# Local attention over smaller score tiles: 8 heads by 16 queries by 48 positions

## The reference, cut to what matters

```
idx = 1 + arange(t_pad)[:, None] + arange(L)[None, :]      # L = 32 positions seen by each query
uk, uv = recK[:, :, idx], recV[:, :, idx]                   # E = 4 records per position
Q = einsum('ntc,hdc->nhtd', X, w_Q)                         # H = 8 heads, DK = 64
scores = einsum('nhtd,netld->nhtel', Q, uk) / sqrt(DK)
probs = softmax(scores over the E * L = 128 keys)
Y = einsum('nhtel,netld->nthd', probs, uv)
return Y @ w_O
```

## Time and profile before

| | us |
|---|---|
| span of the profiled execution | 1794.7 |
| median of 3 runs | 1796.14 (1792.08 to 1797.33) |
| PE busy | 1657.5 (92% of the span) |
| PEld busy | 1273.5 (71%) |
| DVE busy | 1000.5 (56%) |
| ACT busy | 643.1 (36%) |
| POOL busy | 509.4 (28%) |

### The profile page before, as it was taken

One profiled execution on the slowest core, in us unless ns is written; L12 is line 12 of the kernel. 1 busy time (PEld: TensorE's weight loads), 2 busy tenths in 40 slices (PEclk: granted clock), 3 DMA queues, 4 the chain that ended last, 5 costly groups with the idle time before them and its releaser, 6 DMA issues. The chain is left out here.

```text
span 1794.7 us, 31966 instructions
## 1 busy us (share of the span) xinstructions
PE 1657.5 (92%) x10524; PEld 1273.5 (71%) x10524; DVE 1000.5 (56%) x2537; ACT 643.1 (36%) x1913; POOL 509.4 (28%) x655
## 2 busy tenths in 40 slices
PE   8999899999999987778789999998999997999998
PEld 6777677777778755667678888886666665656555
DVE  6545457777777877896632222216888885322221
ACT  3333255554545465345521111112444443111110
POOL 3222210000000066785243333315444441100000
PEclk9999899999999999889789999999999998999999
DMA  7776500000000000000423333312111100000000
GB/s 192 133 150 114 99 13 13 13 13 14 12 12 1 2 16 1 17 24 32 149 54 96 108 107 100 94 53 97 31 30 32 30 24 1 12 12 12 23 12 24
DMA packets 92269, 88.53 MB, mean 49 GB/s; under 512 B 11456, under 2 KB 82048, under 8 KB 91776
## 3 DMA queue, kind: packets, MB, share of 16 engines
q1 hardware_dynamic: 73392, 56.63, 13.2%
q0 software_dynamic: 6912, 18.88, 3.9%
q10 hardware_dynamic: 11856, 11.66, 1.9%
HBM read 46.64 MB, written 23.20 MB: 39 GB/s over the span
## 5 line engine op out<-in xcount | busy, mean ns | idle before, releaser
L845 ACT ACTIVATE probs<-psS,nm 128x256 f32<-128x256 f32 x256 | 119.1, 470 | 182.4 <-DVE nm L878 182.4
L1790 DVE COPY YE<-e_psY 128x512 f32<-128x512 f32 x40 | 27.7, 691 | 227.7 <-PE e_psY L1738 227.7
L1728 PE MATMUL e_psH<-e_XT,w 128*128 128x256 f32 x640 | 144.8, 379 | 0.0
L1738 PE MATMUL e_psY<-w,e_HT 128*128 128x256 f32 x640 | 144.5, 379 | 0.0
L876 DVE TENSOR_REDUCE mx<-psS 128x2 f32<-128x512 f32 x128 | 87.8, 686 | 84.2 <-PE psS L766 81.9
L1738 PEld LDWEIGHTS e_psY<-w,e_HT 128*128 128x128 f32 x640 | 121.6, 190 | 16.5
L766 PE MATMUL psS<-Rec,QT 128*128 128x256 f32 (+1 forms) x512 | 132.3, 381 | 0.9 <-ACT QT L833 0.9
L1766 ACT ACTIVATE e_HT<-e_psH 128x512 f32<-128x512 f32 x80 | 47.7, 597 | 235.9 <-PE e_psH L1728 235.9
L1728 PEld LDWEIGHTS e_psH<-e_XT,w 128*128 128x128 f32 x640 | 118.6, 190 | 14.5
L1696 POOL DMA_INDIRECT XE<-token_rows,held x80 | 76.0, 950 | 184.7 <-PE e_psX L1715 167.3
L1023 POOL TENSOR_TENSOR prodS<-QKV 128x256 f32<-128x256 f32 x112 | 85.5, 793 | 128.4 <-ACT QKV L1195 113.7
(11 more groups left out here) (286 smaller groups left out, 3557.4 us busy)
## 6 DMA issues: line engine op xcount, KB each, us to landing
KD<-KV SPq DMA_DIRECT2D x256, 66.0 KB, 2.5
expert_out<-YE ACTq DMA_DIRECT2D x40, 256.0 KB, 2.1
w<-in_w SPq DMA_DIRECT2D x16, 512.0 KB
X<-in_x SPq DMA_DIRECT2D x8, 512.0 KB, 6.6
x_turned<-XT SPq DMA_DIRECT2D x32, 128.0 KB, 2.3
XS<-x_turned SPq DMA_DIRECT2D x8, 512.0 KB, 4.0
token_rows<-o_XN SPq DMA_DIRECT2D x32, 128.0 KB, 1.7
out_x<-X SPq DMA_DIRECT2D x8, 512.0 KB, 2.9
```

The costliest lines, as they stand in the source:

```text
L845: nc.scalar.activation(probs[:, b.q % 4, hg, :], psS[b.q % 2][:, hg, :], ACT.Exp, bias=nm[:, b.q % 2, hg:hg + 1], scale=scale, accum_out=s ...
L1728: mm = pe.matmul(psH[c % 2][half][:, m, :], w1[:, s, kc, f:f + P], XT[:, c % 2, kc, :], start=(m == 0 and kc == 0), stop=(m == 1 and kc == ...
L1738: mm = pe.matmul(psY[c % 2][:, j, :], HT[:, c % 2, m, j * P:(j + 1) * P], w2[:, s, m, :], start=(j == 0 and m == 0), stop=(j == 1 and m == ...
```

## The change

The score tile of a block is cut in another way. It was 4 heads x 32 queries over 64 positions, twice (head groups). It becomes 8 heads x 16 queries over 48 positions, twice (query halves u = 0 and 1). So a block has 2 x 192 score columns in place of 2 x 256. The 384 columns of probabilities are three transposes of 128 in place of four. The middle one holds the last 16 positions of half 0 in its rows 0 to 63 and the first 16 positions of half 1 in its rows 64 to 127. The value matmuls stay as they were (two key tiles of 32 positions by two head groups), so `PT` keeps 512 columns: DVE copies the first and third transposes (256 columns) and writes the middle one twice through a product with `half`, a constant of ones and zeros, which zeroes the rows that don't belong (256 columns).

The layout of `QT` changes with it (blocks of 16 queries, all heads side by side), and so does the constant selection and mask data, in the same sizes. DVE sets `half` with four small memsets at the head of the stage. POOL's `fetch` and `cover` wait for the same semaphores as before but are issued from the unrolled steps, with one more wait for its own `cover`.

```diff
-        self.QT = [k.sb(ctx, f"QT{r}", [P, 2, NQ, 4, L0]) for r in range(2)]
+        self.QT = [k.sb(ctx, f"QT{r}", [P, T // QUERIES, H0, QUERIES]) for r in range(2)]
...
-        probs = k.sb(ctx, "probs", [P, 4, 2, E0 * KW])
-        PT = k.sb(ctx, "PT", [P, 2, 2, 2, P])
+        probs = k.sb(ctx, "probs", [P, 4, 2, KEYS])
+        PT = [k.sb(ctx, f"PT{x}", [P, 2 * (2 * P + QUERIES)]) for x in range(2)]
...
+            def fetch_next(t):
+                pool.wait_ge(b_ready, t * MADE + (LAST_V + 1 - MADE))
+                pool.wait_ge(masked, t)
+                pass_gate(k, pool)
+                fetch(t)
+            def cover_next(t):
+                pool.wait_ge(r_ready, t + 1)
+                pass_gate(k, pool)
+                cover(t)
+                pool.wait_ge(masked, t + 1)
+            def step(j, s, late):
+                if late < 0 or not isinstance(j, int) or j < NB // 2 - 1:
+                    b = At(j, s, 0)
+                    if late >= 0 and b.q == NQ - 3:
+                        fetch_next(b.t + 2)
+                    if late >= 0 and b.q == NQ - 1:
+                        cover_next(b.t + 2)
...
-                for hg in range(2):
-                    mm = pe.matmul(psS[b.q % 2][:, hg, :], QT[b.r][:, hg, b.q, :, :].rearrange("d h t -> d (h t)"),
-                                   k.Rec[:, bass.ds(b.t, 1), b.q * QB:b.q * QB + KW, :].rearrange("d a t e -> d (a t e)"),
-                                   start=(hg == 0), stop=(hg == 1), skip_group_check=True)
+                for u in range(2):
+                    first = b.q * QB + u * QUERIES
+                    mm = pe.matmul(psS[b.q % 2][:, u, :], QT[b.r][:, b.q * 2 + u, :, :].rearrange("d h t -> d (h t)"),
+                                   k.Rec[:, bass.ds(b.t, 1), first:first + SEEN, :].rearrange("d a t e -> d (a t e)"),
+                                   start=(u == 0), stop=(u == 1), skip_group_check=True)
...
-                for hg in range(2):
-                    for kt in range(2):
-                        mm = pe.transpose(psP[b.q % 2][:, hg, kt, :], probs[:, b.q % 4, hg, kt * P:(kt + 1) * P], k.ident[:, :])
+                both = probs[:, b.q % 4, :, :].rearrange("p u c -> p (u c)")
+                for n in range(2 * KEYS // P):
+                    mm = pe.transpose(psP[b.q % 2][:, n, :], both[:, n * P:(n + 1) * P], k.ident[:, :])
...
-                        ins = nc.scalar.copy(QT[r][0:DK, pair // 2, blocks, 2 * pair % 4 + x, :],
-                                             bank[x * DK:(x + 1) * DK, 0:T // 2].rearrange("d (b t) -> d b t", b=NQ // 2))
+                        ins = nc.scalar.copy(QT[r][0:DK, half * NQ:(half + 1) * NQ, 2 * pair + x, :],
+                                             bank[x * DK:(x + 1) * DK, 0:T // 2].rearrange("d (b t) -> d b t", b=NQ))
...
+            for u in range(2):
+                nc.vector.memset(half[0:HALF, u:u + 1], float(u)).then_inc(half_set, 1)
+                nc.vector.memset(half[HALF:P, u:u + 1], float(1 - u)).then_inc(half_set, 1)
+            dve.wait_ge(half_set, 4)
...
+            def rows_of(x, first, apart):
+                return PT[x][:, first:first + 2 * apart].rearrange("p (k n t) -> p k n t", k=2, t=QUERIES)[:, :, 0:2 * H0 - 1:2, :]
             def turned(b):
...
-                nc.vector.tensor_copy(PT[:, b.q % 2, :, :, :], psP[b.q % 2][:, :, :, :]).then_inc(p_evac, 1)
+                nc.vector.tensor_copy(rows_of(x, 0, 2 * P + QUERIES),
+                                      psP[x][:, 0:3:2, :].rearrange("p k (h t) -> p k h t", t=QUERIES))
+                mixed = psP[x][:, 1, :].rearrange("p (h t) -> p h t", t=QUERIES).unsqueeze(1)
+                nc.vector.tensor_tensor(rows_of(x, QUERIES, 2 * P - QUERIES), bc(mixed, [P, 2, H0, QUERIES]),
+                                        bc(half[:, :].unsqueeze(2).unsqueeze(2), [P, 2, H0, QUERIES]), ALU.mult).then_inc(p_evac, 1)
```

More of the change, by code:

```diff
@@ L34 @@
 WIN = L0 + T
+QUERIES = P // H0
+SEEN = QUERIES + L0
 NH, NKV, HD = 16, 4, 16
@@ L631, in window_attention @@
     NQ = T // QB
-    KW = 2 * L0
+    KEYS = E0 * SEEN
+    HALF = P // 2
     SP2 = 2 * NQ
@@ L661, in window_attention @@
         psB = k.ps(ctx, "psB", [P, 512])
+        half = k.sb(ctx, "half", [P, 2])
+        half_set = k.sem(ctx, "w_half_set")
         r_ready, masked = k.sem(ctx, "w_r_ready"), k.sem(ctx, "w_masked")
@@ L724, in _ @@
             cover(0)
[L725 to L732, removed]
+            pool.wait_ge(masked, 1)
+            fetch_next(1)
+            cover_next(1)
+            turns(pool, step, 0)
         @block.tensor
@@ L843, in exponentials @@
                 act.wait_ge(p_ready, b.g + 1)
-                for hg in range(2):
-                    nc.scalar.activation(probs[:, b.q % 4, hg, :], psS[b.q % 2][:, hg, :], ACT.Exp,
-                                         bias=nm[:, b.q % 2, hg:hg + 1], scale=scale,
-                                         accum_out=sums[:, b.q % 4, hg:hg + 1]).then_inc(e_done, 1)
+                for u in range(2):
+                    nc.scalar.activation(probs[:, b.q % 4, u, :], psS[b.q % 2][:, u, :], ACT.Exp,
+                                         bias=nm[:, b.q % 2, u:u + 1], scale=scale,
+                                         accum_out=sums[:, b.q % 4, u:u + 1]).then_inc(e_done, 1)
             def turned(b):
@@ L906, in step @@
                 if b1 := lagging(j, s, late, 1):
-                    normed(b1)
+                    inverted(b1)
                 if b2 := lagging(j, s, late, 2):
@@ L2497, in lay_out @@
     c["ident"] = np.eye(P, dtype=np.float32)
-    q, s = np.arange(32)[:, None], np.arange(64)[None, :]
-    at = np.concatenate([np.broadcast_to(s, (32, 64)), np.broadcast_to((s - L0) % 64, (32, 64))])
-    q = np.concatenate([q, q])
+    phases = DK // QUERIES
+    row, s = np.arange(DK)[:, None], np.arange(DK)[None, :]
+    q, at = row % QUERIES, (s - row // QUERIES * QUERIES) % DK
     seen = (at > q) & (at <= q + L0)
     c["mask"] = f(np.repeat(np.where(seen, 0.0, NEG).astype(np.float32), E0, axis=1))
-    sel = np.zeros((2, 32, 2, T // 64, 2, 4, 32), np.float32)
-    for odd in range(2):
-        sel[odd, :, :, :, odd, :, :] = np.eye(32, dtype=np.float32)[:, None, None, None, :]
-    c["sel"] = f(sel.reshape(64, -1))
+    sel = np.zeros((phases, QUERIES, T // QUERIES, H0, QUERIES), np.float32)
+    for b in range(T // QUERIES):
+        sel[b % phases, :, b, :, :] = np.eye(QUERIES, dtype=np.float32)[:, None, :]
+    c["sel"] = f(sel.reshape(DK, -1))
     col = lambda v: f(v.reshape(KC, P).T)
```

24 lines of the change are left out of this document (11 added, 13 removed).

## The result

| | before | after |
|---|---|---|
| median, us | 1796.31 (1792.08 to 1797.33, 4 runs) | 1769.26 (1765.17 to 1771.51, 4 runs) |
| ratio | | 0.9849, 95% interval 0.983 to 0.9868 |
| span of the profiled execution | 1794.7 | 1769.0 |
| first to last scores of the local attention | 387.95 | 355.08 |
| last scores to the issue of the next stage's first load | 11.12 | 11.06 |

The change makes the kernel 27 us faster; 1763.3 was forecast, within 1755 to 1776. The touched stage gave what the sum said: the next stage issues its first load 32.9 us earlier (at 600.4 in place of 633.3), and the sum was 32.8. But the span is only 25.7 shorter: in the profiled execution 7.2 us were lost again behind the stage, in code that is the same. That execution took 1770.8 us; the other three of this kernel took 1765.2, 1767.7 and 1771.5.

A forecast was written before the change was run, and what follows sets the result against it. PE, column by column, was taken to set the local attention, except waits behind POOL and in sequence 7. Savings of 3.5, 20.8, 5.1, 3.2 and 0.2 made 32.8 us: span 1761.9, median 1763.3, range 1755 to 1776.

The forecast's parts named there:

- the sum: Local attention stage: savings of sequences 0 to 7 and the drain together 32.8 us, span 1794.7 to 1761.9.
- A PE step: Local attention, each PE step: narrower score passes save 0.215 us, one transpose fewer 0.11, together 0.32.
- The rival that weight loads bind: Score passes on PE: loads at 0.19 us limit the gain to 0.21 a step, 21 us, 1775; chance 0.08.
- A DVE step: Local attention, DVE without waits: 2.16 us a step becomes 2.02; the split costs 0.09, the narrower tile gives 0.23.
- The rival of a dear product: DVE's turned pair: both halves at 0.86 us make the pair 1.57, DVE the bound, 1811; DVE slower has chance 0.03.
- the prediction's estimate from the fixed part of each instruction: DVE's turned pair: 120 cycles per instruction give 0.78 us against 0.66, 0.13 more a step in place of 0.09.
- PE stays in front with 0.4 to spare: Worst pair of steps, `add` then a short one: DVE's turned pair ends at 5.3 us, values due at 5.7.
- POOL's stretch: Steps 13 to 15 of sequences 0 to 5, behind POOL's copies: 0.96 us of the gain lost from each sequence.
- PE waits about 1.4 in place of 0.9: Behind POOL's copies: PE, 0.32 us faster a step, arrives earlier and waits about 1.4 us in place of 0.9.
- Steps 13, 14 and 15 save nothing: Sequences 0 to 5, behind POOL's copies: these three steps gain nothing, 3 x 0.32 = 0.96 us lost from each.
- Sequence 7: Last sequence, where PE stands for DVE at every fourth step: 0.8 us saved per round, 3.2 instead of 5.1.
- The one behind starts on X and new loads, so it moves as a whole: Stage behind the local attention: starts on X and new loads, so it moves as a whole.

The follow-up runs named there:

- the 256 columns: The changed kernel with score products of 256 columns in place of 192, of which 192 are read: 1783.86 us.
- the extra DVE copy: The changed kernel with one more DVE copy of 256 columns per block, from psP to a spare tile: 1782.51 us.
- the fourth transpose: The changed kernel with a fourth transpose per block, its result read by nobody: 1773.16 us.
- the shift: The changed kernel with 20 tiny matmuls on PE behind the last step of the local attention: 1764.5 us.
- the small loads first: The changed kernel with ln1w and ln1b issued ahead of wqkv at the head of the attention over positions: 1766.43 us.
- the last version: The changed kernel with copies of R and the mask by DMA from sequence 2 on, plus 20 tiny matmuls behind PE's last step: 1752.35 us.
- pieces and shift: The changed kernel with POOL's copy of R and mask copy cut in four pieces each, plus 20 tiny matmuls behind PE's last step: 1753.85 us.

## Why the prediction was right, and which step failed

**A PE step.** 0.32 was forecast and 0.32 measured (2.95 to 2.63). The parts hold alone too: passes 0.213, transpose 0.11. The rival that weight loads bind is refuted.

**A DVE step.** 2.02 forecast. A step without waits after, against the earlier trace rows:

```profile
413.45 0.55 DVE L901 TENSOR_REDUCE mx<-psS 128x2 f32<-128x384 f32 x1
...
414.79 0.42 DVE L921 COPY PT<-psP 128x256 f32<-128x256 f32 x1
415.12 0.41 DVE L924 TENSOR_TENSOR PT<-psP,half 128x256 f32<-128x256 f32 x1
```

1.67 us from the maximum's start to the product's, and 0.33 until a next one would start: 2.00. The rival of a dear product is refuted, and the prediction's estimate from the fixed part of each instruction (the Trainium skill, "VectorE: DVE Perf Modes", section on the TRN2 errata), 0.78 for the pair, stood over the measured 0.67 (0.33 from the copy's start to the product's, and as much again); the measurement decides. "PE stays in front with 0.4 to spare" was too generous: 0.34 more a step cost 16 us.

**POOL's stretch.** "PE waits about 1.4 in place of 0.9" came true: 1.37 in the rows, in each of six sequences. "Steps 13, 14 and 15 save nothing" was nearly so: they went from 10.06 to 9.93, so 0.13. A whole sequence (1 to 3, 5) saved 4.33 for 4.16. In sequence 4 it was 3.80. Its second step, 3.78 long before and 3.98 after, got no shorter. DVE stands idle ahead of the sequence's first maximum for nothing that the profile shows, before (2.3 us) and after:

```profile
418.01 0.56 DVE L901 TENSOR_REDUCE mx<-psS 128x2 f32<-128x384 f32 x1 [2.47 <-issue]
```

PE then waits 0.95 us for the scalings in the second step (0.60 before). Sequence 4 is where the hardware loop over pairs of sequences jumps back; that the jump is what holds DVE fits, and is not shown. What I did not weigh is that the wait behind POOL is worth 10 us once PE is faster: the versions without it have a local that is 9.7 to 12.1 shorter.

**Sequence 7.** Its four-step round was to lose 0.8 from 10.85; it went from 10.83 to 10.04.

**The sum** for the stage was 32.8, and 32.9 was measured at the next stage's first issue. That it fits so closely is in part luck, since small misses cancel: sequences 1 to 3 and 5 gave 0.17 more each, sequence 4 0.36 less, and sequence 0, the 15 steps of sequence 7 and the drain 0.1 to 0.2 less each.

**"The one behind starts on X and new loads, so it moves as a whole"**: this step failed. The stage behind did not move as a whole. In the profiled execution it lost 4.6 us in its head and 2.6 further on.

The runs show the cause of the head's first part: a load of instructions beside the stage's own small loads goes with ln1b 2 us late, and PE waits. In six traces the 16 KB packet lies beside the loads in the old order (after, its repeat, POOL's copies by DMA, in pieces, the 256 columns, the extra DVE copy): ln1b lands after 4.1 to 4.6 us and the first product comes 6.46 to 7.12 us behind the issue. In six it does not (before, its repeat, the fourth transpose, the three with the shift): ln1b lands after 2.5 to 3.0, and the first product comes after 5.21 to 5.41 in five of them, after 6.51 in the one whose clock fell ahead of it. The trace does not name the engine whose program is loaded, but two edits of PE's program alone move the packet: it starts 2.8 and 3.05 us behind the issue in the two traces of the changed kernel, 8.1 ahead of it with the fourth transpose, and 2.5 ahead with the shift. Its start is not set by PE's code alone: with the small loads first it comes at 601.4 in place of 603.4, and PE's program is the same.

The clock is a second part, and it doesn't follow from the late load alone: it fell to half in the head in four of the six traces, and stayed at 1.00 with the 256 columns and with the extra DVE copy, behind waits of 1.59 and 1.43 us.

The rest is open. From the issue to the end the two traces of the changed kernel lose 7.2 and 8.6 us against before. The other four with the late load lose 1.6 to 2.2, the shifted kernel 0.2, and the last version, without a late load, 1.9. So the late load is worth at most some 2 us at the end of the span, and the other 5 us of these two executions are not shown to come from it.

The median of the four runs is 6 us over the forecast, and that of all eight is 4 over. Up to 2 us of this fit the late load. The rest goes with how the executions of one kernel differ, 1764.7 at a mean clock of 0.968 to 1772.0 at 0.960, and what sets that is not shown.

## What to carry to other kernels

Add up a PE-bound stage column by column, but read where the next engine is late for each kind of step; the sum then came within 0.1 us of 33, with single sequences off by up to 0.4. Before trusting that "the rest only moves", look at what the next stage's head is made of: short loads that PE waits for, with instruction packets beside them, can land up to 2 us later when code ahead of them grows or shrinks. Before a loss is priced from one trace, look where that execution stands among the timed ones. And once PE is faster, look again at the waits that stay, since cutting POOL's copies into pieces or giving them to a DMA was worth a further 11 to 12 us here (medians of the same batch).

## What the runs showed of the hardware that I had not expected

- A program's own loading shows: a 16 KB packet of 0.95 to 1.4 us beside 1 KB loads goes with a landing of 4.1 to 4.6 us in place of 2.5 to 3.0. In the kernel with the small loads first the packet is there too, and wqkv lands after 3.8 for 3.0.
- In all seven traces with the packet beside the loads, one issue of SyncE's close to it takes 1.26 to 1.94 us; in the other six every issue there takes 0.38 to 0.47.
- PE's clock fell to half behind waits of 1.88, 1.55, 1.43 and 1.35 us (after, its repeat, pieces, DMA), and not behind 1.59 and 1.43 us (256 columns, extra copy; the next products took 1.56 in both). In the kernel with pieces and shift it fell with no such wait. What else decides it is open.
- A POOL copy of 2.0 us holds two DVE scalings for 2.19; four copies of a quarter hold them for 1.13 and let PE through. A DVE product with one operand in PSUM beside such a copy takes its usual 0.41.
